# Token order of attention and column order of the dense layers in a four-stage transformer kernel

## The chip, the cores and the metric

The kernel runs on one core of a Trainium2 chip. The metric is the device time of one execution in microseconds. All inputs lie in the chip's memory when it starts, and the result (8 sequences of 512 tokens by 512 features, float32) lies there when it ends.

## What is computed

Four layers follow one another, each on `x` of shape (8, 512, 512): a stencil layer, an attention block with its feed-forward part, an expert layer whose weights are picked by a token of the sequence, and a low-rank correction. Only the second to the fourth matter here; of the stencil nothing changes. Cut to that:

```python
# attention, with a bias for every head and a mask
x = _ln(src) * (1.0 + scale) + shift
q = (x @ Wq + bq).reshape(B, S, 16, 32).transpose(0, 2, 1, 3)      # k, v alike
scores = einsum('bhqd,bhkd->bhqk', q / sqrt(32), k) + attention_bias
scores = where(src_mask, -inf, scores)
ctx = einsum('bhqk,bhkd->bhqd', softmax(scores), v).transpose(0, 2, 1, 3).reshape(B, S, D)
x = x + (ctx @ Wo + bo)
# its feed-forward part: 512 -> 2048 -> 512
h = _ln(x) * g2 + beta2
x = x + (_gelu2(h @ W1 + b1) @ W2 + b2)
# expert layer: the same shape, weights of expert e of the sequence
o = gelu(x @ Wi[e] + bi[e]) @ Wo[e] + bo[e]
y = _ln(o + x) * gamma[e] + beta[e]
# correction: rank 32, with a gate from the mean over the tokens
out = y + strength * ((y @ basis) @ basis.T[:, :32] @ resp_w.T + resp_b + safety_bias)
```

The bias is (8, 16, 512, 512) float32, 134 MB, and is read once. The mask is one byte for each query and key.

## The kernel before

The program has one stage after the other: `stencil`, `attention`, `feed_forward` (expert=False), `feed_forward` (expert=True, with the correction in its `tail`). Each stage writes `x` to memory and the next reads it. Every engine has its own stream of instructions, written out by hand, and they meet by semaphores alone: no scheduler moves anything. P is 128, S and D are 512, R = 4 blocks of tokens, C = 4 blocks of features.

**Token order.** `rows_at` (line 84) loads and stores a sequence as "(p r)": partition p holds tokens 4p to 4p+3, one contiguous run of 8 KB. A transpose on TensorE of block r gives 128 columns, which are tokens r, r+4, r+8 and so on. `by_row` (line 72) is a view of a 512-column tile with a step of 4 elements (16 bytes) between neighbours. Before the change the engines that empty the transposes from PSUM write through it, so that columns stand in the tokens' natural order, and whoever needs the 128 tokens of block r again reads with the step of 4: as the stationary operand of a matmul, or as a transpose's input.

**Attention**, a loop over 8 sequences. `transposes_x` brings x to features by tokens, VectorE writes `xT` with scale and shift (line 1048), ScalarE and VectorE split it into a high part `xH` and a rest `xL` (a product of three fp32r matmuls stands for one in float32: `split_matmul`, lines 91 to 93). Projections q, k, v follow. q and k are made in 4 chunks of 4 heads; SyncE copies each head's high and low parts into `q3` and `k3`, 96 partitions deep. Then come 64 units (u), each one head and one block r of 128 queries, 16 units to a chunk:

- `scores` (TensorE, line 875): one matmul, the stationary operand is `by_row(q3)` of block r, 96x128, moving `k3`, 512 columns. It is issued two units ahead.
- GpSimd has added the mask to the bias of two units (line 723); SyncE loads the bias of two units, 512 KB, in one transfer (line 649) into one of four buffers.
- `sum_scores` (VectorE, line 993), `exp` (ScalarE, line 775), four transposes (TensorE, line 883), `probs_high` (ScalarE, line 782), `probs_low` (VectorE, line 999), `values` (TensorE, line 896, for two units at once).

At unit 8 of the next chunk (u = 24, 40, 56, and after the last unit) the finished chunk is closed: `ctx_high` (ScalarE, line 797) writes `cH` and `ctx_low` (VectorE, line 1025) writes `cL`, both with the step of 4; ScalarE's next instructions, `copy_low` (line 791) and with it the `exp` behind, wait for `cL`. After the units come the output projection, its transposes back (line 942, input `by_row(xT)`) and the store.

In the middle of a sequence, when the second chunk of q and k is being copied, `prefetch` loads x (1 MB) and the mask (256 KB) of the next sequence through the same queue.

**feed_forward**, again 8 sequences of 16 steps f. `transposes` fill PSUM, `h_out` (ScalarE, lines 1450 and 1452) writes `h32` with the step of 4 (by_row), VectorE splits it. A step is `hidden` (12 matmuls, stationary weights) and `output` of the step before (12 matmuls into four banks; the stationary operand is block r of `gH` or `gL`, read with the step of 4). In the expert stage the `tail` of the sequence before runs along: transposes of y (line 1582), `yH` (ScalarE, line 1472) and `yL` (VectorE, line 1821), both written with the step of 4, and the last matmuls (line 1605) with `feats` read with the step of 4. Transposes m and m+1 use one bank, so transpose m+1 waits for `yL` m.

## Time and profile before

| | us |
|---|---|
| median of 3 runs | 3721.76 |
| lowest, highest | 3713.49, 3722.09 |
| the profiled execution | 3728.08 |
| its span, first to last instruction | 3726.3 |
| mean granted clock of TensorE | 0.921 |
| TensorE busy (matmuls) | 3054.0, 82% |
| TensorE weight loads | 2531.2, 68% |
| VectorE busy | 2138.4, 57% |
| ScalarE busy | 1225.2, 33% |
| GpSimd busy | 895.2, 24% |
| DMA | 352.04 MB, 94 GB/s |

The stencil takes the first 225 us, attention goes to 1940 us, the first feed_forward to 2745 us, the expert stage to the end.
### The profile page before, as it was taken

What the parts mean: (1) busy time and instruction counts of PE and PEld (TensorE: products, weight loads), DVE (VectorE), ACT (ScalarE), POOL (GpSimd) and SP (SyncE); (2) the same over time, 40 slices, a digit from 0 to 9 for tenths busy, and PEclk for the clock granted to TensorE, in tenths of its full rate; (3) what the DMA queues carried; (4) which work ended last, traced back from release to release, by engine and by line L of the source; (5) the groups of instructions that cost most, each with busy time, mean ns of one, the idle gap of its engine ahead of it and who ended that gap; (6) DMA issues with size and microseconds to landing.
All of it is one profiled execution on the core that took longest, in us unless ns stands there. A gap on an engine that the chain in (4) does not pass through costs nothing. (4 is left out here: it accounts for less than half of the span.)

```text
span 3726.3 us, 45793 instructions
## 1 busy us (share of the span) xinstructions
PE 3054.0 (82%) x14000; PEld 2531.2 (68%) x14000; DVE 2138.4 (57%) x3930; ACT 1225.2 (33%) x2286; POOL 895.2 (24%) x573
## 2 busy tenths in 40 slices
PE   7938787777777787778769999999979898889886
PEld 4426666666666566666658888988867787778775
DVE  8946667575756667575754444334346465545543
ACT  1116556463636455464611111111111121121121
POOL 1013424142424324242421000000023122211210
PEclk9969899888989899889989999999979999999997
DMA  4235344342525344443422000000034323323310
GB/s 147 95 109 153 111 136 140 117 139 80 159 89 158 97 136 128 128 142 105 139 89 63 23 23 12 11 23 23 12 103 142 102 83 99 102 88 100 94 52 28
DMA packets 204298, 352.04 MB, mean 94 GB/s; under 512 B 25546, under 2 KB 100234, under 8 KB 199306
## 3 DMA queue, kind: packets, MB, share of 16 engines
q1 hardware_dynamic: 202330, 345.96, 30.1%
q0 software_dynamic: 1712, 2.93, 0.3%
q8 instruction: 127, 2.08, 0.2%
q14 instruction: 129, 1.06, 0.1%
HBM read 264.45 MB, written 34.01 MB: 80 GB/s over the span
## 5 line engine op out<-in xcount | busy, mean ns | idle before, releaser
L723 POOL TENSOR_TENSOR at_bias<-at_bias,at_mask 128x1024 f32<-128x1024 f32 x256 | 556.4, 2182 | 1034.2 <-DMA at_bias<-in_fside_Bx16xSxS 1033.8
L883 PE MATMUL at_bank_probT<-at_ident,at_y 128*128 128x128 f32 x2048 | 349.6, 298 | 174.5 <-ACT at_y L775 174.2
L993 DVE CUSTOM_DVE_ANT_0 at_bias<-at_bias,at_bank_score 128x512 f32<-128x512 f32 x512 | 349.6, 684 | 244.1 <-PE at_bank_score L875 146.2
L775 ACT ACTIVATE at_y<-at_bias,at_nmax 128x512 f32<-128x512 f32 x512 | 369.3, 721 | 272.0 <-DVE at_nmax L993 269.1
L883 PEld LDWEIGHTS at_bank_probT<-at_ident,at_y 128*128 128x128 f32 x2048 | 266.6, 153 | 259.6 <-ACT at_y L775 231.9
L896 PE MATMUL at_bank_ctx<-at_pH,at_v 128*64 128x256 f32 x1024 | 291.0, 313 | 104.2 <-DVE at_pL L999 100.0
L999 DVE TENSOR_TENSOR at_pL<-at_bank_probT,at_pH 128x512 fp32r<-128x512 f32 x512 | 352.5, 688 | 28.2 <-ACT at_pH L782 24.5
L875 PE MATMUL at_bank_score<-at_k,at_q 96*128 96x512 f32 x512 | 314.2, 616 | 15.4 <-DMA at_k<-at_nat 15.4
L782 ACT ACTIVATE at_pH<-at_bank_probT 128x512 fp32r<-128x512 f32 x512 | 300.7, 587 | 70.5 <-PE at_bank_probT L883 67.2
L1704 DVE CAST ff_gH<-ff_g 128x512 fp32r<-128x512 f32 x128 | 68.2, 532 | 437.4 <-ACT ff_g L1460 437.2
L1460 ACT ACTIVATE ff_g<-ff_bank_hid,ff_b1c 128x512 f32<-128x512 f32 x128 | 88.2, 689 | 657.8 <-PE ff_bank_hid L93 657.8
L1460 ACT ACTIVATE expert_g<-expert_bank_hid,expert_b1c 128x512 f32<-128x512 f32 x128 | 88.2, 689 | 654.2 <-PE expert_bank_hid L93 654.2
L1386 POOL TENSOR_SCALAR expert_WH<-expert_stage 128x1024 fp32r<-128x1024 f32 x128 | 148.9, 1163 | 611.9 <-PE expert_bank_out L93 476.7
L896 PE MATMUL at_bank_ctx<-at_pL,at_v 128*64 128x256 f32 x1024 | 279.5, 302 | 0.0
L896 PEld LDWEIGHTS at_bank_ctx<-at_pH,at_v 128*64 128x64 f32 x1024 | 150.8, 147 | 180.8 <-DVE at_pL L999 121.1
L1704 DVE CAST expert_gH<-expert_g 128x512 fp32r<-128x512 f32 x128 | 66.6, 520 | 302.8 <-ACT expert_g L1460 302.8
L91 PE MATMUL expert_bank_out<-expert_WH,expert_gH 128*128 128x512 f32 x512 | 210.8, 412 | 13.5 <-DVE expert_gL L1706 13.5
L91 PE MATMUL ff_bank_hid<-ff_hH,ff_WH 128*128 128x512 f32 x512 | 208.1, 407 | 7.0 <-DVE ff_hL L1698 2.6
L91 PE MATMUL expert_bank_hid<-expert_hH,expert_WH 128*128 128x512 f32 x512 | 204.8, 400 | 6.1 <-DVE expert_hL L1698 4.1
L92 PE MATMUL expert_bank_out<-expert_WL,expert_gH 128*128 128x512 f32 x512 | 205.4, 401 | 0.0
L91 PE MATMUL ff_bank_out<-ff_WH,ff_gH 128*128 128x512 f32 x512 | 204.9, 400 | 0.0
L93 PE MATMUL expert_bank_out<-expert_WH,expert_gL 128*128 128x512 f32 x512 | 204.5, 400 | 0.0
(306 smaller groups left out, 6887.4 us busy)
## 6 DMA issues: line engine op xcount, KB each, us to landing
at_bias<-in_fside_Bx16xSxS SPq DMA_DIRECT2D x256, 512.0 KB, 4.2
expert_stage<-in_L_cond_Wi SPq DMA_DIRECT2D x128, 256.0 KB, 2.8
expert_stage<-in_L_cond_Wo SPq DMA_DIRECT2D x128, 256.0 KB, 2.9
at_q<-at_nat SPq DMA_DIRECT2D x384, 64.0 KB, 2.0
at_k<-at_nat SPq DMA_DIRECT2D x384, 64.0 KB, 2.6
st_f<-in_x SPq DMA_DIRECT2D x8, 1024.0 KB, 7.4
x_after_layer<-st_y SPq DMA_DIRECT2D x8, 1024.0 KB, 4.8
at_x<-x_after_layer SPq DMA_DIRECT2D x8, 1024.0 KB, 8.0
```

Source lines behind the costliest of these rows:

```text
L91: pe.matmul(out, wh, xh, start=first, stop=False)
L92: pe.matmul(out, wh, xl, start=False, stop=False)
L93: return pe.matmul(out, wl, xh, start=False, stop=last)
L723: pool.tensor_tensor(bias[i % NB][:, :, :], bias[i % NB][:, :, :], mask[:, 2 * i % R:2 * i % R + 2, :], ALU.add).then_inc(s_bm, 1)
L775: act.activation(prob[u % 2][:, :], bias[u // 2 % NB][:, u % 2, :], ACT.Exp, scale=-1.0, bias=nmax[:, u % 4:u % 4 + 1], accum_out=sums[:, ...
L782: act.activation(pH[u // 2 % 2][:, :, u % 2, :], pT[u % 2][:, :].rearrange("p (k q) -> p k q", q=P), ACT.Copy).then_inc(s_pth, 1)
L875: pe.matmul(pS[u % 2][:, :], by_row(q3[:, j, :])[:, r, :], k3[:, j, :], start=True, stop=True).then_inc(s_qk, 1)
L883: t = pe.transpose(pT[u % 2][:, k * P:(k + 1) * P], prob[u % 2][:, k * P:(k + 1) * P], ident[:, :])
L896: t = pe.matmul(pC[h % 2][0:2 * HD, half * 2 * P:(half + 1) * 2 * P], v[:, k, h, :], probs[i % 2][:, k], start=(k == 0 and g == 0), stop=( ...
L993: dve.tensor_tensor_reduce(t, t, pS[u % 2][:, :], -1.0, 3.0e38, ALU.add, ALU.min, nmax[:, u % 4:u % 4 + 1]).then_inc(s_max, 1)
L999: dve.tensor_tensor(pL[u // 2 % 2][:, :, u % 2, :], pT[u % 2][:, :].rearrange("p (k q) -> p k q", q=P), f32(pH[u // 2 % 2][:, :, u % 2, :] ...
L1460: act.activation(g32[f % 2][:, :], pg[f % 2][:, :], ACT.Gelu if expert else ACT.Gelu_apprx_sigmoid, bias=b1c[:, slot if expert else 0, f:f ...
```

## The change

Attention takes its tokens in another order: `tokens_at` loads and stores x as "(r p)", so that partition p of block r holds token 128r + p. The bias and the mask, whose query rows lie on the same partitions, are loaded in the same order. A transpose of block r then gives 128 columns that already are the tokens' natural order, and all views with a step of 4 in attention become plain slices.

`feed_forward` keeps loading and storing by `rows_at`. Its columns now stay as the transposes leave them, block after block, instead of being put in natural order; since every later step takes whole blocks, nothing else depends on the order. Here too all views with the step become plain slices.

No instruction is added, removed or moved on any engine: each of the five has the same rows in the same order before and after. What differs is the steps in the operands of these instructions, and the pieces of these transfers: the bias moves in 2 KB pieces instead of 4 KB, x of attention in 2 KB instead of 8 KB, the mask in 512-byte pieces instead of 2 KB. The number of bytes stays. Line numbers after line 88 grow by 5, and by 4 and 3 near the end.

```diff
+def tokens_at(x, n):
+
+    return x[ds(n, 1)].rearrange("a (r p) n -> (a p) r n", r=R)
...
-                    sp.dma_start(x[:, :, :], rows_at(x_in, 0)).then_inc(s_x, 16)
-                    sp.dma_start(m8[:, :, :], a["mask_Bx1xSxS_bk0"][0].rearrange("a (p r) k -> (a p) r k", r=R)).then_inc(s_m8, 16)
+                    sp.dma_start(x[:, :, :], tokens_at(x_in, 0)).then_inc(s_x, 16)
+                    sp.dma_start(m8[:, :, :], a["mask_Bx1xSxS_bk0"][0].rearrange("a (r p) k -> (a p) r k", r=R)).then_inc(s_m8, 16)
...
-                sp.dma_start(bias[i % NB][:, :, :], a["fside_Bx16xSxS_0"][ds(n, 1), h].rearrange("a (p r) k -> (a p) r k", r=R)[:, r:r + 2, :]).then_inc(s_bias[i % NB], 16)
+                sp.dma_start(bias[i % NB][:, :, :], a["fside_Bx16xSxS_0"][ds(n, 1), h].rearrange("a (r p) k -> (a p) r k", r=R)[:, r:r + 2, :]).then_inc(s_bias[i % NB], 16)
...
-                sp.dma_start(rows_at(x_out, n), y[:, :, :]).then_inc(s_st, 16)
+                sp.dma_start(tokens_at(x_out, n), y[:, :, :]).then_inc(s_st, 16)
...
-                act.activation(by_row(cH[:, c, :]), pv[:, :].rearrange("d (r p) -> d r p", r=R), ACT.Identity,
+                act.activation(cH[:, c, :], pv[:, :], ACT.Identity,
...
-                pe.matmul(pS[u % 2][:, :], by_row(q3[:, j, :])[:, r, :], k3[:, j, :],
+                pe.matmul(pS[u % 2][:, :], q3[:, j, r * P:(r + 1) * P], k3[:, j, :],
...
-                        t = pe.transpose(out[:, m * P:(m + 1) * P], by_row(xT[:, m, :])[:, r, :], ident[:, :])
+                        t = pe.transpose(out[:, m * P:(m + 1) * P], xT[:, m, r * P:(r + 1) * P], ident[:, :])
...
-                dve.scalar_tensor_tensor(by_row(cL[:, c, :]), pv[:, :].rearrange("d (r p) -> d r p", r=R), bc[:, 3, c:c + 1],
-                                         by_row(f32(cH[:, c, :])), ALU.add, ALU.subtract).then_inc(s_cl, 1)
+                dve.scalar_tensor_tensor(cL[:, c, :], pv[:, :], bc[:, 3, c:c + 1],
+                                         f32(cH[:, c, :]), ALU.add, ALU.subtract).then_inc(s_cl, 1)
...
-                    dve.tensor_scalar(by_row(xT[:, m, :]), pJ[m % 2][:, :].rearrange("d (r p) -> d r p", r=R),
+                    dve.tensor_scalar(xT[:, m, :], pJ[m % 2][:, :],
...
-                    out = by_row(h32[m % 2][:, :])
-                    src = pt[m % 2][:, :].rearrange("d (r p) -> d r p", r=R)
+                    out, src = h32[m % 2][:, :], pt[m % 2][:, :]
...
-                    act.activation(by_row(yH[m % 2][:, :]), pt[0][:, :].rearrange("d (r p) -> d r p", r=R), ACT.Identity,
+                    act.activation(yH[m % 2][:, :], pt[0][:, :], ACT.Identity,
...
-                    gh = gH[f % 2][:, :].rearrange("d (p r) -> d r p", r=R)[:, r, :]
-                    gl = gL[f % 2][:, :].rearrange("d (p r) -> d r p", r=R)[:, r, :]
+                    gh = gH[f % 2][:, r * P:(r + 1) * P]
+                    gl = gL[f % 2][:, r * P:(r + 1) * P]
...
-                    ft = feats[:, :].rearrange("d (p r) -> d r p", r=R)[:, r, :]
+                    ft = feats[:, r * P:(r + 1) * P]
...
-                    dve.tensor_tensor(by_row(yL[m % 2][:, :]), pt[0][:, :].rearrange("d (r p) -> d r p", r=R),
-                                      by_row(f32(yH[m % 2][:, :])), ALU.subtract).then_inc(s_yl, 1)
+                    dve.tensor_tensor(yL[m % 2][:, :], pt[0][:, :], f32(yH[m % 2][:, :]), ALU.subtract).then_inc(s_yl, 1)
```

The transfers of the next sequence's x and mask in `prefetch` change in the same way as the first ones.

## Rows read from the trace of the kernel before

**Rows 1.** Stretches: length, busy time by engine, TensorE's clock, DMA share, GB/s.

```profile
225.00:1940.00 1715.00, 1289.79 (x6625) 1038.55 (x6626) 1107.79 (x2167) 883.85 (x1837) 605.20 (x301) 0.88 0.42 126
1940.00:2745.00 805.00, 753.92 (x3384) 683.08 (x3384) 331.38 (x796) 120.51 (x155) 84.59 (x76) 0.98 0.09 29
2745.00:3726.00 981.00, 829.02 (x3545) 722.28 (x3545) 522.18 (x730) 187.23 (x275) 193.30 (x143) 0.93 0.29 90
```

**Rows 2.** Weight loads by line and form: busy us, mean ns, idle before.

```profile
L875 PEld LDWEIGHTS at_bank_score<-at_k,at_q 96*128 96x128 f32 x512 | 159.3, 312 | 19.2 <-DMA at_k<-at_nat 18.9
...
L92 PEld LDWEIGHTS ff_bank_out<-ff_WL,ff_gH 128*128 128x128 f32 x512 | 158.6, 310 | 0.1
...
L92 PEld LDWEIGHTS ff_bank_hid<-ff_hL,ff_WH 128*128 128x128 f32 x512 | 98.9, 193 | 20.0
```

**Rows 3.** Timeline, first feed_forward: start us, us, engine, line; first matmuls of series.

```profile
2206.74 0.40 PE L91 MATMUL ff_bank_hid<-ff_hH,ff_WH 128*128 128x512 f32 x1
...
2209.47 0.40 PE L91 MATMUL ff_bank_out<-ff_WH,ff_gH 128*128 128x512 f32 x1
...
2212.29 0.40 PE L91 MATMUL ff_bank_hid<-ff_hH,ff_WH 128*128 128x512 f32 x1
```

**Rows 4.** VectorE's and ScalarE's groups by line and form, columns as in Rows 2.

```profile
L1025 DVE SCALAR_TENSOR_TENSOR at_cL<-at_y,at_bc,at_cH 128x512 fp32r<-128x512 f32 x32 | 57.8, 1806 | 10.3 <-ACT at_cH L797 10.1
L981 DVE SCALAR_TENSOR_TENSOR at_nat<-at_bank_proj,at_bc,at_nat 128x512 fp32r<-128x512 f32 x64 | 47.9, 749 | 75.5 <-ACT at_nat L764 75.5
...
L1048 DVE TENSOR_SCALAR at_xT<-at_bank_proj,at_adab 128x512 f32<-128x512 f32 x32 | 36.5, 1181 | 16.4 <-issue 12.9 <-PE at_bank_proj L841 3.3 <-DVE at_adab L1040 0.2
...
L1821 DVE TENSOR_TENSOR expert_yL<-expert_bank_tr,expert_yH 128x512 fp32r<-128x512 f32 x32 | 34.8, 1087 | 11.9 <-ACT expert_yH L1472 11.9
...
L764 ACT ACTIVATE at_nat<-at_bank_proj,at_bc 128x512 fp32r<-128x512 f32 x64 | 43.9, 685 | 76.6 <-PE at_bank_proj L93 76.6
L797 ACT ACTIVATE at_cH<-at_y,at_bc 128x512 fp32r<-128x512 f32 x32 | 38.9, 1216 | 12.3 <-DVE at_y L1021 12.3
...
L1450 ACT ACTIVATE expert_h<-expert_bank_tr 128x512 f32<-128x512 f32 x32 | 33.8, 1122 | 94.0 <-PE expert_bank_tr L1530 91.3 <-DVE expert_hL L1698 2.7
```

**Rows 5.** Timeline where the first chunk of sequence 3 is closed.

```profile
962.98 2.14 POOL L723 TENSOR_TENSOR at_bias<-at_bias,at_mask 128x1024 f32<-128x1024 f32 x1 [2.37 <-DMA at_bias<-in_fside_Bx16xSxS]
963.14 2.92 DVE L1025 SCALAR_TENSOR_TENSOR at_cL<-at_y,at_bc,at_cH 128x512 fp32r<-128x512 f32 x1
...
966.64 0.70 ACT L775 ACTIVATE at_y<-at_bias,at_nmax 128x512 f32<-128x512 f32 x1
```

**Rows 6.** The instructions of line 1025: duration ns min/median/max, starts.

```profile
L1025 DVE SCALAR_TENSOR_TENSOR at_cL<-at_y,at_bc,at_cH x32: 1129/1158/2977, 348.4 to 1873.5; 128x512 fp32r<-128x512 f32 x32
```

**Rows 7.** Timeline: a matmul of 512 columns that follows small ones, twice.

```profile
999.79 0.60 PE L875 MATMUL at_bank_score<-at_k,at_q 96*128 96x512 f32 x1
...
2201.07 0.48 PE L91 MATMUL ff_bank_hid<-ff_hH,ff_WH 128*128 128x512 f32 x1
```

**Rows 8.** Who waited for the matmuls of line 875: us, times.

```profile
  DVE at_bias L993: 146.2, 147
```

**Rows 9.** Timeline, start of a sequence: VectorE's first two `xT`.

```profile
1086.10 2.20 DVE L1048 TENSOR_SCALAR at_xT<-at_bank_proj,at_adab 128x512 f32<-128x512 f32 x2 [3.24 <-issue]
```

**Rows 10.** Timeline: transposes that waited for what empties their bank.

```profile
2020.12 0.66 PE L1530 MATMUL ff_bank_tr<-ff_ident,ff_xn 128*128 128x128 f32 x4 [0.91 <-ACT ff_h L1452]
...
3144.27 0.66 PE L1582 MATMUL expert_bank_tr<-expert_ident,expert_x 128*128 128x128 f32 x4 [1.30 <-DVE expert_yL L1821]
...
3702.16 1.12 PE L1582 MATMUL expert_bank_tr<-expert_ident,expert_x 128*128 128x128 f32 x4 [2.25 <-DVE expert_yL L1821]
```

**Rows 11.** Transfers by tile: count, KB each, median us from issue to landing.

```profile
at_bias<-in_fside_Bx16xSxS SPq DMA_DIRECT2D x256, 512.0 KB, 4.2
expert_stage<-in_L_cond_Wi SPq DMA_DIRECT2D x128, 256.0 KB, 2.8
expert_stage<-in_L_cond_Wo SPq DMA_DIRECT2D x128, 256.0 KB, 2.9
```

More of the change, by code:

```diff
@@ L666, in prefetch @@
                 sp.sem_inc(s_passed, 1)
-                sp.dma_start(x[:, :, :], rows_at(x_in, n + 1)).then_inc(s_x, 16)
-                sp.dma_start(m8[:, :, :], a["mask_Bx1xSxS_bk0"][ds(n + 1, 1)].rearrange("b a (p r) k -> (b a p) r k", r=R)).then_inc(s_m8, 16)
+                sp.dma_start(x[:, :, :], tokens_at(x_in, n + 1)).then_inc(s_x, 16)
+                sp.dma_start(m8[:, :, :], a["mask_Bx1xSxS_bk0"][ds(n + 1, 1)].rearrange("b a (r p) k -> (b a p) r k", r=R)).then_inc(s_m8, 16)
             steps = [(2 * (i - NB) + 2.5, load_bias, (i,)) for i in range(NB, NP)]
```

## The prediction, made before the change was run

> **What bounds the kernel now.** I read the stretches first, then the groups by form, then timelines where one engine waits. The two feed_forward stages belong to TensorE: in the first it is busy for 754 of 805 us at a clock of 0.98 [rows 1], and matmuls follow one another without a break. Attention takes 1715 us, 46% of the span, and there no engine is full (TensorE 75%, VectorE 65%, ScalarE 52%) [rows 1]: it is a chain that passes from engine to engine within a unit. A stride thus costs something only where its instruction sets the pace (feed_forward) or where the chain stands still until it has ended (attention).
>
> **What the step of 4 costs one instruction.** The trace has each kind both ways. A weight load of 128 columns with the step takes 310 ns (312 for the scores), without it 193 [rows 2]. VectorE writes `xT` from PSUM in 1181 ns, while line 981 does the like without the step in 749; ScalarE takes 1216 ns for `cH` and 1122 for `h32`, and 685 for line 764 [rows 4]. So I take 120 ns off a load, 0.43 us off `xT` and 0.5 us off ScalarE's instructions. For `yL` (1087 ns) and `cL` I take 0.4 us. All ends of the terms below start from these.
>
> The Trainium skill (SBUF — State Buffer, Door 1) says that SBUF has lines of 16 bytes and that an access which crosses into a new one each time pays. It also calls a stride of 4 float32 free, which would leave all of this at zero and the time at that of before; the pairs above speak for the first half of its sentence.
>
> **1. feed_forward, `output`.** Twelve `hidden` matmuls start at 2206.74 and the first `output` one at 2209.47: 2.73 us. The twelve of `output` take from there to 2212.29: 2.82 us [rows 3]. The load with the step lies behind the matmul before it except for 0.09/12 = 7.5 ns. 256 steps f of twelve: 256 x 0.09 = 23 us. 24 of the steps wait for `yL` and lose nothing by this; 22 us remain. Bounds: 0 (the pace comes from the change of bank and not from the load) and 23.
>
> **2. Closing a chunk.** 32 times `cH`, then `cL`, and in 24 of them `exp` waits behind; in the other 8 the output projection does. `cL` takes 1158 ns in the median, but 1806 on average [rows 4, 6]; 32 x 0.65 = 21 us are thus in the few that take up to 2977. The timeline shows what these are: GpSimd began its mask sum at 962.98, `cL` at 963.14, it took 2.92 us, and `exp` came at 966.64 [rows 5]. With `cH` shorter by 0.5, `cL` begins at 962.6, ahead of GpSimd, whose start hangs on a transfer. Then such a `cL` costs 0.75 instead of 2.92, 2.2 us less. 21/1.8 = 11.5, so 11 of the 32 are of this kind: 11 x (0.5 + 2.2) = 30 us, the other 21 x (0.5 + 0.4) = 19 us. Together 49. Bounds: 32 x 0.4 = 13 us if every `cL` still ends with GpSimd's sum, and 49.
>
> The Trainium skill (SBUF — State Buffer, Who interferes with whom) has it that a VectorE instruction with two SBUF inputs and a GpSimd one that reads SBUF exclude each other for the whole of the one that began first. By that rule it is the order of the two starts, not the stride, that decides, as in the sum above; where `cL` still comes second, the rule gives back the lower bound.
>
> **3. Scores.** After small matmuls a load isn't covered: the record of `scores` is 0.60 us, that of a 512-column matmul without the step in the same position 0.48 [rows 7]. 0.12 us for each of 512 at most: 61 us. But it counts only where VectorE waits for the scores, and it did 147 times [rows 8]; elsewhere VectorE or ScalarE is behind. 147 x 0.12 = 18, less those at the half clock, where a load is covered more easily (clock 0.88 on average, so about a quarter of attention [rows 1]): 14 us. Bounds: 0 and 61.
>
> **4. Start of a sequence.** `xT` 0 and 1 take 2.20 us back to back [rows 9], and `xT` 2 too lies ahead of the q projection, whose bank it frees: 3 x 0.43 x 8 = 10 us. The fourth is hidden by the projection at half clock. Bounds 0 and 14.
>
> **5. Turns between sequences in feed_forward.** The third transpose waited 0.91 us for ScalarE's `h32`, the fourth alike [rows 10]: with 0.5 less each, 1 us x 8 in the first stage, and half of it in the second, where transposes run at the half clock: 12 us. Three transposes of y in a sequence wait 1.30 us for `yL` [rows 10], which is last behind the split of gelu and of the weights on VectorE; `yH` is done earlier. 21 x 0.4 = 8 us. After the last sequence nothing covers the chain, transposes wait 2.25 us [rows 10]: 4 x (0.5 + 0.4) = 4 us. Together 24, bounds 12 and 24.
>
> **6. The transposes of the output and `feats`** read without the step too: some 2 us, bounds 0 and 5.
>
> **7. Transfers.** Pieces get smaller, bytes stay. The nearest rows: 256 KB in 512-byte pieces (`Wi`) land in 2.8 us, 256 KB in 2 KB pieces (`Wo`) in 2.9 [rows 11]. So the mask and the bias should take no longer. They matter where VectorE waits for a bias, above all behind the 1.25 MB of `prefetch`, 7 times; I put 0.4 us each against the change, 3 us, since the long pieces of x have no counterpart. Bounds: 0, and the price in the last rival.
>
> **Sum**: 22 + 49 + 14 + 10 + 24 + 2 - 3 = 118 us. The profiled execution took 3728.1, so 3610; the median of the runs is 6.3 us below it, so **3604** for the median. The clock is left as it is: shorter stalls in attention should not lower it.
>
> **Rivals.**
> - *The loop gives it back.* GpSimd still comes first at `cL`, the scores' 0.12 us end in VectorE's own work and the smaller pieces cost double. Then terms 2, 3 and 7 are 13, 0 and -8: 22 + 13 + 10 + 24 + 2 - 8 = 63 us, **3659**. For it speaks that VectorE and ScalarE are busy for half of attention, and that both starts hang on the same `exp`; against it, that the lead of GpSimd was 0.16 us and `cH` loses three times that.
> - *TensorE is the chain in every unit.* Then the scores give all of 61 instead of 14 and `xT` 14: 118 + 47 + 4 = 169 us, **3553**. For it: VectorE waited for scores in more than a quarter of the units, and the transposes and `values` behind them in TensorE's queue move too. Against it: `exp` and `probs_low` are more often what TensorE waits for.
> - *The stride isn't the cause*, and the change does not do what it is said to: loads and writes stay as long since another property of these instructions makes them slow. The pairs in rows 2 and 4 differ in tiles too. Time as before, **3722**.
> - *Slower: small pieces stop the SyncE queue.* Copies of q and k share it with the bias. From 256 to 512 KB a landing grows by 4.2 - 2.9 = 1.3 us [rows 11], so 512 KB hold the queue for 2.6. If a byte costs twice as much in small pieces, the three bias transfers among the copies of each of 24 chunks add 7.8 us, and `prefetch` adds 6.4 us 7 times: 187 + 45 = 232 us, less the 118: **3836**. It turns to slower once a byte costs half as much again. Against it stands that `Wi`'s 512-byte pieces are no slower than `Wo`'s.
>
> **How the numbers follow.** Forecast 0.58 (3580 to 3635), the loop gives it back 0.22, TensorE in every unit 0.12, stride not the cause 0.03, slower 0.03, and 0.02 for a gain between 0 and 40 us. To hold 8 in 10 the range takes in the forecast and the first rival and reaches towards the second: **3560 to 3670**. About 0.3% (11 us) is what a measurement of this kernel can tell from no change. Faster by more: 0.94. Within: 0.03. Slower: 0.03.
>
> **What would show it.** Weight loads of `scores` and of `output` near 190 ns, and twelve `output` matmuls in 2.73 us: term 1. `cH` at 0.7, `cL` at 0.75 with hardly any above 2 us: term 2; if the long ones stay in number, the first rival. VectorE's wait for the scores down by 14 us or by far more: term 3. `xT` at 0.75, `h32` at 0.6 to 0.7, `yL` at 0.7. Bias landings still near 4.2 us, else the last rival. What would make it wrong is a stall in attention that stands just behind the one removed: the copies of q and k at a chunk's start hold the first units of it, and they don't get shorter; a gain well below 49 us in the sequences' loops with all durations as said would mean that.

## The result and the profile after

| | before | after |
|---|---|---|
| median of four runs, us | 3721.93 | 3616.76 |
| lowest, highest | 3713.49, 3722.40 | 3610.97, 3633.11 |
| profiled execution | 3728.08 | 3619.43 |

The ratio is 0.973 with a 95% interval of 0.9695 to 0.9765: 105 us less, where 118 had been forecast and 3604 us for the median. The time lies 13 us above the forecast and inside its range of 3560 to 3670.

Where it went, by stage. A stage runs here from its first GpSimd instruction to that of the next (the cuts in rows 1 were rounder: the first 46 us of feed_forward stood in attention's stretch). Columns: stretch, length, busy time of TensorE, its weight loads, VectorE, ScalarE and GpSimd (with instructions), TensorE's granted clock, DMA share, GB/s. The kernel before:

```profile
224.90:1893.60 1668.70, 1262.96 (x6528) 1016.23 (x6528) 1083.23 (x2133) 875.83 (x1829) 583.04 (x279) 0.89 0.42 126
1893.60:2730.60 837.00, 776.69 (x3456) 702.35 (x3456) 354.16 (x824) 127.15 (x161) 97.98 (x77) 0.97 0.10 31
2730.60:3726.30 995.70, 833.08 (x3568) 725.34 (x3568) 523.96 (x736) 188.60 (x276) 202.14 (x163) 0.93 0.29 92
```

and the changed kernel:

```profile
225.90:1833.60 1607.70, 1176.57 (x6528) 933.75 (x6528) 1058.60 (x2133) 858.51 (x1829) 579.31 (x280) 0.91 0.45 130
1833.60:2650.60 817.00, 763.50 (x3456) 628.43 (x3456) 353.94 (x824) 113.75 (x161) 98.25 (x78) 0.97 0.11 32
2650.60:3617.70 967.10, 814.64 (x3568) 647.13 (x3568) 514.32 (x736) 160.31 (x276) 200.71 (x163) 0.93 0.30 94
```

Attention lost 61 us, feed_forward 20, the expert stage 28.6. The groups of the changed kernel that answer to rows 2 and 4 (busy us, mean ns of one, idle time before them and its cause):

```profile
L880 PEld LDWEIGHTS at_bank_score<-at_k,at_q 96*128 96x128 f32 x512 | 105.5, 206 | 22.0 <-DMA at_k<-at_nat 21.4
...
L97 PEld LDWEIGHTS ff_bank_out<-ff_WL,ff_gH 128*128 128x128 f32 x512 | 96.2, 188 | 19.9
...
L1030 DVE SCALAR_TENSOR_TENSOR at_cL<-at_y,at_bc,at_cH 128x512 fp32r<-128x512 f32 x32 | 38.5, 1204 | 6.3 <-ACT at_cH L802 6.3
...
L1019 DVE COPY at_y<-at_inv 128x512 f32<-128x512 f32 x32 | 29.1, 908 | 1.1
...
L1053 DVE TENSOR_SCALAR at_xT<-at_bank_proj,at_adab 128x512 f32<-128x512 f32 x32 | 25.1, 804 | 17.9 <-issue 17.5 <-PE at_bank_proj L846 0.2 <-DVE at_adab L1045 0.2
...
L802 ACT ACTIVATE at_cH<-at_y,at_bc 128x512 fp32r<-128x512 f32 x32 | 22.9, 715 | 12.3 <-DVE at_y L1026 12.3
L1825 DVE TENSOR_TENSOR expert_yL<-expert_bank_tr,expert_yH 128x512 fp32r<-128x512 f32 x32 | 21.9, 684 | 10.4 <-ACT expert_yH L1476 10.4
```

Loads went from 312 and 310 ns to 206 and 188, `cH` from 1216 to 715, `xT` from 1181 to 804, `yL` from 1087 to 684: what a single instruction saves was forecast to within 0.06 us. Only `cL` stands out, with a mean of 1204 where 750 was expected. Its instructions by duration (min/median/max in ns) show that the typical one is short and the long ones are still there:

```profile
L1030 DVE SCALAR_TENSOR_TENSOR at_cL<-at_y,at_bc,at_cH x32: 740/750/2734, 348.4 to 1813.6; 128x512 fp32r<-128x512 f32 x32
```

By the timeline 7 of them take more than 2 us; there were 11.

### The profile page after: what moved, and what is told of

It reads as the page before. It is cut to its first block and busy times, and to the rows that moved or that the text cites. A ratio compares the mean times of both kernels' runs of the same rounds, so it can differ in the third digit from the quotient of the medians.

```text
span 3617.7 us, 45793 instructions
## 1 busy us (share of the span) xinstructions
PE 2936.1 (81%) x14000; PEld 2296.7 (63%) x14000; DVE 2104.3 (58%) x3930; ACT 1166.1 (32%) x2286; POOL 890.2 (25%) x573
## 5 line engine op out<-in xcount | busy, mean ns | idle before, releaser
L998 DVE CUSTOM_DVE_ANT_0 at_bias<-at_bias,at_bank_score 128x512 f32<-128x512 f32 x512 | 348.8, 682 | 215.6 <-PE at_bank_score L880 124.7
L880 PE MATMUL at_bank_score<-at_k,at_q 96*128 96x512 f32 x512 | 258.8, 508 | 17.8 <-DMA at_k<-at_nat 17.7
L96 PE MATMUL expert_bank_hid<-expert_hH,expert_WH 128*128 128x512 f32 x512 | 204.2, 399 | 7.0 <-DVE expert_hL L1702 4.7
L98 PE MATMUL ff_bank_hid<-ff_hH,ff_WL 128*128 128x512 f32 x512 | 204.6, 400 | 0.0
L97 PE MATMUL ff_bank_hid<-ff_hL,ff_WH 128*128 128x512 f32 x512 | 204.3, 399 | 0.0
```

The lines of the kernel that those rows point to most:

```text
L96: pe.matmul(out, wh, xh, start=first, stop=False)
L97: pe.matmul(out, wh, xl, start=False, stop=False)
L98: return pe.matmul(out, wl, xh, start=False, stop=last)
L880: pe.matmul(pS[u % 2][:, :], q3[:, j, r * P:(r + 1) * P], k3[:, j, :], start=True, stop=True).then_inc(s_qk, 1)
L998: dve.tensor_tensor_reduce(t, t, pS[u % 2][:, :], -1.0, 3.0e38, ALU.add, ALU.min, nmax[:, u % 4:u % 4 + 1]).then_inc(s_max, 1)
```

## Why GpSimd still came first

The prediction said that with `cH` shorter by 0.5 us `cL` would begin 0.5 us earlier. The kernel before, at the place of rows 5, shows what that left out:

```profile
961.88 1.23 ACT L797 ACTIVATE at_cH<-at_y,at_bc 128x512 fp32r<-128x512 f32 x1
...
962.54 0.69 DVE L999 TENSOR_TENSOR at_pL<-at_bank_probT,at_pH 128x512 fp32r<-128x512 f32 x1
```

`cH` ends at 963.11, but VectorE itself is busy with the `pL` that stands ahead of `cL` in its queue, and `cL` follows it at 963.14. Two things hold `cL`, and they end together. In the changed kernel at the same place only the queue is left:

```profile
936.15 0.71 ACT L802 ACTIVATE at_cH<-at_y,at_bc 128x512 fp32r<-128x512 f32 x1
...
936.69 0.69 DVE L1004 TENSOR_TENSOR at_pL<-at_bank_probT,at_pH 128x512 fp32r<-128x512 f32 x1
937.29 2.71 DVE L1030 SCALAR_TENSOR_TENSOR at_cL<-at_y,at_bc,at_cH 128x512 fp32r<-128x512 f32 x1
...
937.31 2.14 POOL L728 TENSOR_TENSOR at_bias<-at_bias,at_mask 128x1024 f32<-128x1024 f32 x1 [2.79 <-DMA at_bias<-in_fside_Bx16xSxS]
...
940.59 0.70 ACT L780 ACTIVATE at_y<-at_bias,at_nmax 128x512 f32<-128x512 f32 x1
```

`cH` is done at 936.86 and `cL` begins 0.43 us later. It loses to GpSimd although its record begins 0.02 us earlier. One sequence on, the lead is 0.06 us and it wins; now GpSimd's sum takes 2.69 us instead of 2.14:

```profile
1133.91 0.74 DVE L1030 SCALAR_TENSOR_TENSOR at_cL<-at_y,at_bc,at_cH 128x512 fp32r<-128x512 f32 x1
...
1133.97 2.69 POOL L728 TENSOR_TENSOR at_bias<-at_bias,at_mask 128x1024 f32<-128x1024 f32 x1 [3.55 <-DMA at_bias<-in_fside_Bx16xSxS]
```

The rule of the Trainium skill (SBUF — State Buffer, Who interferes with whom), that whoever starts first has the shared port for the whole instruction, agrees with both places if a lead of 0.02 us in the records is taken as a tie.

## The experiments

For the parts of attention I compare with the mean of three profiles in which attention is the same (the changed kernel, `dense_old` and `output_step4`: 1607.7, 1619.1 and 1605.4 us, mean 1610.7). An effect below some 10 us in a single stage time of attention is thus not told, and the kernel before has one profile to compare with, 1668.7 us. The feed_forward stages repeat better: 812.5 to 819.0 and 963.6 to 970.0 us over all kernels in which they are as changed. "Loops" is the sum over 8 sequences from the first `exp` to the end of the last, "between" the sum of the 7 stretches from there to the next sequence's first `exp`.

### Which part gives what, taken back one at a time

**dense_old**: the whole `feed_forward` function of the kernel before, attention as changed.

> Attention as changed, both feed_forward stages as before the change; the output is the reference's. If the stages do not influence each other, attention stays at 1607.7, the stages go back to 837.0 and 995.7, and the whole takes 48.6 us more than the changed kernel, 3668. If the time of attention moves by more than 2 us here, stage times can't be compared that finely between profiles.

Measured: 3671.24 us, ratio to before 0.9883 (0.9848 to 0.9919), 54 us above the changed kernel; stages 1619.1, 831.5 and 990.4. Over the four kernels with the old dense stages these take 835.3 and 991.8 us on average, with the new ones 814.9 and 967.1: the dense part is worth 20.4 + 24.7 = 45 us by the stages. Attention moved by 11 us with nothing changed in it, which the text had named as the sign that single stage times there can't be read to 2 us.

**output_step4**:

```diff
-                    gh = gH[f % 2][:, r * P:(r + 1) * P]
+                    gh = gH[f % 2][:, :].rearrange("d (p r) -> d r p", r=R)[:, r, :]
```

and `gl` alike.

> The changed kernel with only the stationary operand of output, in both feed_forward stages, read with the step of 4 again; the rows of the output are then other tokens than those of x. Term 1: 0.09 us in each of 256 steps, 11.5 us in each stage but for the 24 steps of the second that wait for yL: the stages at 828.5 and 977.5 us from 817.0 and 967.1. If the load is hidden and the change of bank makes the pace: within 1 us of 817.0 and 967.1.

Measured (one run): 830.9 and 970.5 us, so 16.0 and 3.4 us against those means, 19.4 together where 22 was forecast. The 3.4 us lie just outside the spread of that stage, so that the split between the stages is rough. The load, back at 310 ns, isn't fully hidden in either stage: the starts of neighbouring `output` matmuls are 237 ns apart in the median in both, against 227 in the changed kernel. In the first the price is larger than forecast, in the second most of it disappears: there TensorE waits in other places as well. That a slower `output` shortens those waits is my reading; no run shows it by itself.

**scores_step4**, **xT_step4** and **close_step4**: one view with the step back in each.

```diff
-                pe.matmul(pS[u % 2][:, :], q3[:, j, r * P:(r + 1) * P], k3[:, j, :],
+                pe.matmul(pS[u % 2][:, :], by_row(q3[:, j, :])[:, r, :], k3[:, j, :],
...
-                    dve.tensor_scalar(xT[:, m, :], pJ[m % 2][:, :],
+                    dve.tensor_scalar(by_row(xT[:, m, :]), pJ[m % 2][:, :].rearrange("d (r p) -> d r p", r=R),
...
-                act.activation(cH[:, c, :], pv[:, :], ACT.Identity,
+                act.activation(by_row(cH[:, c, :]), pv[:, :].rearrange("d (r p) -> d r p", r=R), ACT.Identity,
```

(in `close_step4` also `cL`).

> The changed kernel with only the scores' stationary operand read with the step of 4 again, so the rows of the scores belong to other tokens than the bias. Term 3 of the forecast: the weight load goes back from 206 to about 310 ns and attention gets 14 us longer (1622). If TensorE is the chain in every unit: 61 us or more (1669). If the wait ends in VectorE's own queue: attention stays within 3 us of 1607.7.

> The changed kernel with only xT written with the step of 4 again, so that q, k and v have their tokens in another order than the bias. Term 4 of the forecast: three of the four count, 0.43 us each, 8 times: 10 us, attention 1618. If all four count and the projections behind them also run at the lower clock for longer: 14 us and more. Between the loops, the stretch from the first to the last xT took 5.43 before and 4.32 us after.

> The changed kernel with only cH and cL written with the step of 4 again, so the output projection has its columns in another order than xT. If each closing stands in the path with its whole length: cH 0.5 and cL 0.4 longer in 32 closings, 29 us, and attention 1637. If cL still ends with GpSimd's sum where it comes second, in 8 of them, and those lose only 0.5: 25 us. If as much as the forecast's term 2, with three more collisions: 36 us, 1644. A stall behind it that takes the time up (the bias behind the prefetch, in the chunk where 8 of the closings stand): 15 us or less.

**pieces_4k**: `rows_at` instead of `tokens_at`, "(p r)" for the bias and the mask.

> The changed kernel with attention's five transfers in the old order (token p*4+r on partition p, pieces of 4 KB for the bias, of 8 KB for x and y); everything on the engines is as changed. The bias and mask then belong to other tokens than the scores. Theory 1, the small pieces cost time behind the prefetch: VectorE's wait for the bias of the second chunk's fourth unit, which grew from 6.13 to 7.24 us in sequence 3, goes back to about 6.1, and attention gets 7 to 9 us shorter than the 1607.7 us of the changed kernel. Theory 2, that wait is set by the bytes in the queue and grew only because the loop now reaches it earlier: attention stays at 1607.7 within 2 us, the wait stays near 7.2 us. The forecast had put 3 us on the pieces.

| kernel | time, us | attention, against 1610.7 | loops, against 1178.5 | between, against 340.6 | `cL` over 2 us |
|---|---|---|---|---|---|
| changed kernel | 3616.8 | -3 | -3 | -1 | 7 |
| scores_step4 | 3632.0 | +11 | +12 | -1 | 10 |
| xT_step4 | 3645.7 (one run) | +24 | +8 | +13 | 5 |
| close_step4 | 3663.3 | +47 | +31 | +15 | 13 |
| pieces_4k | 3633.1 | +6 | +8 | -2 | 11 |
| all of attention (kernel before) | | +58 | +27 | +28 | 11 |

The closing costs 47 us when it is taken back, about the 49 of term 2 and more than any reading of the expectation allowed (36 at most). The scores cost 11 (15 by the medians) against 14, and TensorE isn't the chain in every unit. `xT` costs 24 in its one profile instead of 10. The small pieces do not cost anything that is seen here: with the old ones attention is not shorter, and the medians are 16 us longer. The first theory asked for a wait near 6.1 us in sequence 3 and got 6.3 instead of 7.2, but with the small pieces that wait is 5.3 us in `dense_old` and 7.4 in `output_step4`, so it tells nothing. But the four add up to 88 us, and all together are worth 58. In the stretches between loops they add (13 + 15 = 28), in the loops they do not (59 against 27).

### The same parts added to the kernel before

**old_close_plain** and **old_scores_plain**: the edits of `close_step4` and `scores_step4` the other way round, on the kernel before.

> The kernel before with one part of the change alone: cH and cL written without the step, so the output projection has its columns in another order than xT. Undoing this part in the changed kernel cost 47 us of attention. If the parts add, attention falls from 1668.7 to about 1622 and the time by 47 us. If they overlap in the loops of the sequences (undone one at a time they cost 31, 12 and 8 us there, together they gave 27), whoever comes first takes most: the loops fall from 1205 to 1179 or less and the stretches between them by 15 us, 41 us in all or more, and nothing is left in the loops for the other parts. If the clock is what couples them, half-clock time falls from 372 to about 310 us.

> The kernel before with only the scores' stationary operand read without the step; the rows of the scores belong to other tokens than the bias. Undone in the changed kernel this part cost 11 us of attention, 15 us of the median. If the parts add: attention 1655 to 1658. If a stall of the closings or of the bias takes the time up in the kernel before: attention 1665 to 1672, no gain.

| kernel | time, us | ratio, 95% interval | attention, against 1668.7 | loops | between | `cL` over 2 us |
|---|---|---|---|---|---|---|
| old_close_plain | 3705.5 | 0.9958, 0.9937 to 0.9979 | -26 | -9 | -16 | 13 |
| old_scores_plain | 3710.7 | 0.9973, 0.9947 to 0.9998 | -4 | 0 | -2 | 13 |

For the closing none of my three readings held. Its medians give 15 us, with 8 to 23 in the interval, and the profile 26; neither is 47 or 41, and the time at the half clock in attention fell from 372 to 332 us, not to 310. For the scores the second reading, no gain, holds by the profile (1665.0), while the medians of ten runs give 10 us. Whoever comes first doesn't take most: the closing alone takes 9 us off the loops, while taking it back from the changed kernel costs 31. The timeline shows what stands in its way:

```profile
955.43 2.14 POOL L723 TENSOR_TENSOR at_bias<-at_bias,at_mask 128x1024 f32<-128x1024 f32 x1 [1.54 <-DMA at_bias<-in_fside_Bx16xSxS]
...
955.65 2.47 DVE L1025 SCALAR_TENSOR_TENSOR at_cL<-at_y,at_bc,at_cH 128x512 fp32r<-128x512 f32 x1
```

Here `cH` ends at 955.10, but VectorE gets through its queue only at 955.65, 0.55 us later, since the `sum_scores` ahead of it waits for a matmul with the slow load. GpSimd is 0.22 us ahead. With both parts the lag is 0.43 us and the starts nearly coincide. The slow load is one thing that settles who gets the port at `cL`: in `scores_step4` the lag is 0.55 us too, and all eight first-chunk closings are long (4 to 6 of the eight in the three profiles with the attention as changed). The pieces of the transfers are another, which I had overlooked. In `pieces_4k` the lag is 0.43 us, as in the changed kernel, but GpSimd starts 0.01 to 0.15 us ahead in all eight, and all eight are long; at the same place as above:

```profile
940.51 2.13 POOL L728 TENSOR_TENSOR at_bias<-at_bias,at_mask 128x1024 f32<-128x1024 f32 x1 [1.69 <-DMA at_bias<-in_fside_Bx16xSxS]
...
940.66 2.54 DVE L1030 SCALAR_TENSOR_TENSOR at_cL<-at_y,at_bc,at_cH 128x512 fp32r<-128x512 f32 x1
```

So three parts of the change act on one race. How much the closing and the scores give together on the kernel before was not run. The totals of `cL` are, in us: 57.8 before [rows 4], 48.2 with the closing alone, 38.5, 38.2 and 36.0 in the three profiles with the attention as changed, 41.5 with the scores taken back, 46.1 with the pieces, 61.1 with the closing. Adding `cH` (32 x 0.5 = 16 us each time) gives 16 + 10 = 26 us for the closing alone, which is what its profile says and more than its medians do, and 16 + 23.5 = 39.5 of the 47 for the closing taken back.

With the scores alone the time goes elsewhere. VectorE's waits for scores and for biases together fall from 232.9 to 217.0 us, 16 less, while `cL` takes 4.3 more, the copy of the inverses (line 1014) 6.6 more and the multiplications of line 965 1.8 more.

### Without any collision at cL

**cL_first**:

```diff
+                    if u % UC == 8 and u > UC:
+                        ctx_low(n, u // UC - 1)
                     if u > 0:
                         probs_low(n, u - 1)
                     if u - 1 in after:
                         low(n, after[u - 1])
                     if u % UC == 8 and u > UC:
-                        ctx_low(n, u // UC - 1)
                         add_high(n, u // R - 2)
```

> The changed kernel with one edit of order: in the unit where a chunk is closed, VectorE does cL before the pL of the unit before, so that it begins as soon as cH has ended, some 0.4 us ahead of GpSimd's sum, instead of 0.02 us around it. The output is the reference's. Theory, the order of the two starts decides: no cL above 1.2 us, eight times 2.0 us less, and pL comes 0.8 us later at 24 closings, of which some reaches TensorE: attention 10 to 16 us shorter than 1607.7. Rival 1, the order doesn't decide and any overlap blocks VectorE: eight cL still take 2.6 to 2.7 us. Rival 2, the collision goes but the bias behind the prefetch or the next pL takes the time up: cL short, attention within 3 us of 1607.7.

Measured: 3618.13 us, ratio 0.9712 (0.9671 to 0.9753), the same as the changed kernel; attention 1607.5. No `cL` is long any more, but VectorE's multiplications of `x` by `rstd` (line 970) grow and its wait for GpSimd's sum is longer. `cL_first`, two groups and a wait (us, times, longest):

```profile
L970 DVE TENSOR_SCALAR at_x<-at_x,at_mv,at_rstd 128x512 f32<-128x512 f32 x32 | 30.6, 1018 | 1.2 <-POOL at_rstd L710 1.2
...
L1030 DVE SCALAR_TENSOR_TENSOR at_cL<-at_y,at_bc,at_cH 128x512 fp32r<-128x512 f32 x32 | 25.8, 805 | 9.4 <-ACT at_cH L802 6.5
...
DVE at_bias L998 <- POOL at_bias L728: 90.4, 26, 7.9
```

The changed kernel:

```profile
L970 DVE TENSOR_SCALAR at_x<-at_x,at_mv,at_rstd 128x512 f32<-128x512 f32 x32 | 24.3, 823 | 1.2 <-POOL at_rstd L710 1.2
...
DVE at_bias L998 <- PE at_bank_score L880: 124.7, 114, 6.4
DVE at_bias L998 <- POOL at_bias L728: 79.5, 24, 7.2
```

The first theory holds for the port: the order of the starts decides. For the time rival 2 fits: against the means of the three profiles with the attention as changed, `cL` lost 11.8 us (37.6 to 25.8), while line 970 took 4.5 more (26.1 to 30.6), the copy of line 1019 3.6 more (30.7 to 34.3) and the wait for a bias 7.9 more (82.5 to 90.4). The last is within what these three show among themselves, 79.5, 91.7 and 76.3 us. Taken together with the wait for scores it is 214.7 us against 204.2, 208.5 and 205.0, which is outside. That these put the gain back on the chain isn't shown by them. I looked at the wait for the bias, the largest of the three.

### The stall behind: a bias that comes late

In the changed kernel VectorE stands still in unit 20 of sequence 3 until GpSimd has masked a bias:

```profile
924.83 0.69 DVE L998 CUSTOM_DVE_ANT_0 at_bias<-at_bias,at_bank_score 128x512 f32<-128x512 f32 x1 [7.24 <-POOL at_bias L728]
```

**split_prefetch**: four rows of x and the mask as five transfers, each behind the bias of another unit, instead of `if k == 8` for all of it.

```diff
-                    if k == 8 and not last:
-                        prefetch(n)
+                    if k in parts and not last:
+                        prefetch(n, parts.index(k))
```

with `parts` the steps at units 4, 8, 22, 24 and 38, and **split_cL_first**, the same with `cL` ahead.

> The changed kernel with the prefetch of the next sequence in parts: the four 256 KB rows of x behind the bias of units 4, 8, 22 and 24, the mask behind that of unit 38, instead of 1.25 MB at once near unit 12. The output is the reference's. Theory, the wait of VectorE for the bias in unit 20 of a sequence (4.8 to 7.2 us, 7 times, where the eighth sequence has no prefetch) is this transfer standing ahead of the bias in the queue: it falls to 1 us or less, attention 28 to 40 us shorter than 1611 (mean of three profiles of the same attention), the time near 3585. Rival, the queue is late anyway since copies of q and k hold it: the wait moves to a later unit and attention stays above 1600.

> The split prefetch and cL ahead of pL together; the output is the reference's. cL ahead of pL alone took 12 us out of cL and gave none of it to the whole. If it was the late bias that took it up, it shows here: 8 to 12 us below the split prefetch alone. If it is the order of VectorE's queue itself (pL and values come 0.8 us later in 24 closings), the two kernels are within 3 us of each other.

Measured: 3583.66 us (ratio 0.9633, 0.9595 to 0.967), attention 1577.0, and 3582.97 us (0.9629, 0.9588 to 0.9669), attention 1571.8. The prefetch was the wait of unit 20: it is gone, and with it 33 us of the time, although the copy of the inverses grew from 30.7 to 44.9 us and the wait of unit 18 from 16 to 20. Putting `cL` ahead is worth 1 us by the medians and 5 by the profile, within the noise; my 8 to 12 us failed here too.

What remained were waits in units 18, 34 and 50, where a chunk of q and k has just been copied. SyncE's queue in `split_cL_first` (start, us, with the number of issues):

```profile
888.40 0.37 SPq L655 DMA_DIRECT2D at_bias<-in_fside_Bx16xSxS  x1
892.79 1.79 SPq L665 DMA_DIRECT2D at_q<-at_nat  x3
894.62 1.86 SPq L665 DMA_DIRECT2D at_k<-at_nat  x3
896.52 1.85 SPq L665 DMA_DIRECT2D at_q<-at_nat  x3
898.66 0.38 SPq L655 DMA_DIRECT2D at_bias<-in_fside_Bx16xSxS  x1
```

Between 888.40 and 898.66 no bias is issued. **bias_queue** lets ScalarE issue the bias loads:

```diff
                     if u > 0:
                         probs_high(n, u - 1)
+                    if u % 2 == 1:
+                        i = u // 2 + NB
+                        if i < NP:
+                            load_bias(act, n, i)
+                        elif not last:
+                            load_bias(act, n + 1, i - NP)
```

> The split prefetch with cL ahead of pL, and in addition the bias loads issued by ScalarE in every second unit behind pH, on the same condition as before, instead of by SyncE, whose queue keeps the copies of q and k and the five parts of the prefetch. The output is the reference's. With the split prefetch VectorE still waits for a bias in units 18, 34 and 50 of each sequence (2.7, 3.0 and 2.4 us, 24 times, some 65 us with the copies of the inverses that GpSimd's same sum holds up). Theory, the bias stands behind the copies of q and k in SyncE's queue, which wait for scores: these waits fall below 20 us in all, attention to 1530 or less from 1571.8, the time to 3545 or less. Rival 1, the transfers themselves are what is late there (copies and bias share the engines): the waits stay within a fifth, the time within 10 us of 3583. Rival 2, ScalarE pays for 256 issues, 0.1 us each: 26 us back, the time near 3570.

Measured: **3521.87 us**, ratio to before 0.9447 (0.9407 to 0.9486), the fastest of all; attention 1515.8. Of VectorE's waits for GpSimd's sum, 63.4 us in `split_cL_first`, nothing is left; all that it waits for there is

```profile
DVE at_bias L1010 <- PE at_bank_score L892: 139.0, 156, 2.4
DVE at_bias L1010 <- issue: 9.2, 11, 3.5
DVE at_bias L1010 <- ACT at_y L786: 1.4, 4, 0.4
```

Not all of the 63.4 us is gained: the wait for scores grew from 113.5 to 139.0, and the copy of the inverses fell from 43.5 to 20.8: 63 - 26 + 23 = 60 us, where attention got 56 shorter. The transfers were not late by their bytes but by their place in the queue. The 252 issues take 0.39 us each in ScalarE's records, 98 us in all and not 26 as the second rival had it, and cost nothing that shows in the sum. The same edit gives the prefetch waits of its own, which was not run apart. The Trainium skill (Trainium Kernel Development and Optimization, Key Constraints) says that issuing from several engines saves only the issue time. Here it saves more, since SyncE's queue is taken in order and the copies in it wait for scores.

## Why the prediction was right or wrong, step by step

**The direction and the size** came out: 105 us where 118 was forecast. Of the dense stages' terms, 22 + 24 + about 1, 45 us were measured; of attention's, 49 + 14 + 10 + 2 - 3 = 72, only 58 to 60. That the sum came within 13 us is in part luck: in the loops 27 us were gained where the terms hold 56, and between them 28 where the terms hold some 18.

**Term 1, `output`: 22, measured 19.** The reading from the starts was right; the sum has a slip, since 24 steps of 0.09 less leave 21 and not 22. In the changed kernel twelve `output` matmuls, the next twelve `hidden` and what follows start at the same distance, 2.72 us:

```profile
2090.28 0.39 PE L96 MATMUL ff_bank_out<-ff_WH,ff_gH 128*128 128x512 f32 x1
...
2093.00 0.39 PE L96 MATMUL ff_bank_hid<-ff_hH,ff_WH 128*128 128x512 f32 x1
...
2095.72 0.39 PE L96 MATMUL ff_bank_out<-ff_WH,ff_gH 128*128 128x512 f32 x1
```

Over both stages the price was split 16 to 3, not half to half: in the expert stage more is lost in other waits than the 24 steps that the sum had taken out for it.

**Term 5, turns in feed_forward: 24, measured 26** as what is left of the 45 (with the transposes of y and `feats` in it). TensorE's waits of the expert stage before the change,

```profile
PEld expert_bank_tr L1582 <- DVE expert_yL L1821: 38.9, 24, 3.2
...
PEld expert_bank_tr L1530 <- ACT expert_h L1450: 8.7, 16, 1.0
```

and after it,

```profile
PEld expert_bank_tr L1586 <- DVE expert_yL L1825: 32.4, 24, 2.4
...
PEld expert_bank_tr L1534 <- ACT expert_h L1454: 2.7, 8, 0.5
```

account for 12.5 us of it in that stage, against 4 + 8 + 4 of the sum.

**Term 2, closing a chunk: 49. This is the step that failed**, and in it the sentence "with `cH` shorter by 0.5, `cL` begins at 962.6, ahead of GpSimd". `cH` gave its 16 us. `cL` gave 20 (57.8 to a mean of 37.6) instead of 33: 7 long ones stayed of 11, since VectorE's own queue held `cL` as long as `cH` had. Taken back from the changed kernel the closing costs 47 us (`close_step4`), of which some 9 are TensorE's clock between the sequences and not the instructions; by itself it is worth 26 by the profile and 15 by the medians. By its instructions the closing thus gave 36 us in the changed kernel, 13 less than the term, as much as the sum and the measurement differ by; the surplus of term 4 and a rest in the loops, below, cancel. The first rival had the mechanism (GpSimd still first) and took it for all of them; the truth lies between, nearer to it at first chunks, where 6 of 8 were still long.

**Term 3, scores: 14, measured 11 to 15** in the changed kernel. The attention of `scores_step4`, 1622.1 us, is the 1622 of the expectation. VectorE's wait for the scores fell from 146.2 us [rows 8] to 124.7, but this sign doesn't tell the price: with the slow load back it is 120.6, since the profile puts a wait behind both scores and bias down now to one, now to the other. Both together are 232.9 us before, 205.9 in the mean of the three profiles and 215.0 in `scores_step4`. At the half clock, as the sum had it, the load is covered: the record of a `scores` matmul is 775 ns in the median with the step and without, at full clock 594 and 481. The second rival, 61 us, is out. In the kernel before the same edit gives 4 us in the profile and 10 by the medians.

**Term 4, start of a sequence: 10, measured 24 in one profile, of it 13 between the loops.** The 8 us in the loops are within the noise. The `xT` themselves give 0.38 us each, three or four of them 9 to 12 us. What was missing is TensorE's clock, which the prediction had left as it is. From the last `exp` of sequence 3 to the first of sequence 4 it took, before and after (the last one of a sequence in the first row, the first one of the next in the second):

```profile
1055.69 0.72 ACT L775 ACTIVATE at_y<-at_bias,at_nmax 128x512 f32<-128x512 f32 x1 [0.75 <-DVE at_nmax L993]
...
1111.55 0.72 ACT L775 ACTIVATE at_y<-at_bias,at_nmax 128x512 f32<-128x512 f32 x1 [1.59 <-DVE at_nmax L993]
```

```profile
1026.01 0.72 ACT L780 ACTIVATE at_y<-at_bias,at_nmax 128x512 f32<-128x512 f32 x1 [0.56 <-DVE at_nmax L998]
...
1077.00 0.72 ACT L780 ACTIVATE at_y<-at_bias,at_nmax 128x512 f32<-128x512 f32 x1 [1.59 <-DVE at_nmax L998]
```

55.9 against 51.0 us. The shorter instructions, `cH`, `cL` and four `xT`, explain 0.5 + 0.4 + 1.1 = 2.0 of the 4.9. The rest lies in two places: from the first matmul of the output projection to its last addition (10.7 us before, 9.2 after) and from the first q matmul to the `exp` (21.5 and 19.8). These are the same matmuls at another clock: the first 4 us of the output projection behind `cL` and the first 6 of the q projection behind `xT`, before,

```profile
1065.00:1069.00 4.00, 3.89 (x10) 3.12 (x11) 0.80 (x2) 0.00 (x0) 0.00 (x0) 0.57 0.01 2
1090.00:1096.00 6.00, 5.96 (x15) 4.67 (x16) 2.74 (x4) 1.43 (x3) 0.00 (x0) 0.52 0.00 0
```

and after:

```profile
1034.50:1038.50 4.00, 3.92 (x17) 3.25 (x18) 0.95 (x3) 0.00 (x0) 0.00 (x0) 1.00 0.00 2
1057.20:1063.20 6.00, 5.96 (x22) 4.91 (x23) 3.27 (x5) 1.89 (x3) 0.00 (x0) 0.83 0.00 0
```

At 0.57 and 0.52 nearly all of it ran at 1.2 GHz; after the change the output projection ran at 2.4 GHz throughout (17 matmuls instead of 10 in 4 us) and the q projection rose after a few. What stood ahead of the output projection, before and after:

```profile
1065.11 0.79 PE L91 MATMUL at_bank_proj<-at_cH,at_WH 128*128 128x512 f32 x1 [2.08 <-DVE at_cL L1025]
```

```profile
1034.58 0.50 PE L96 MATMUL at_bank_proj<-at_cH,at_WH 128*128 128x512 f32 x1 [1.22 <-DVE at_cL L1030]
```

TensorE stood still for 2.08 us and for 1.22. `close_step4` brings the slow output projection back in 4 of 7 sequences and `xT_step4` a longer stretch of slow q projection in all, hence 15 and 13 us where 6 and 8 (7 x 0.9 and 7 x 1.1) are in the instructions.

**Terms 6 and 7.** The transposes of the output read without the step too, at 140 ns instead of 210; their 2 us can't be told apart. The pieces were forecast at 3 us lost, and no loss was found: `pieces_4k` is 6 us longer in attention and 16 by the medians, on the other side, with 11 long `cL`. If anything the small pieces helped. The rival on the other side, 3836, is out: the landing of a bias stayed at 4.1 us in the median against 4.2 [rows 11].

**The stride isn't the cause** is out as well: each instruction whose step was put back went back to its old duration. The Trainium skill (SBUF — State Buffer, Door 1) calls a stride of 4 float32 free; on every reader and writer here it cost 0.07 to 0.5 us an instruction, so on that the measurement decides against the sentence. Its 16-byte lines would explain the price; no run here tries another step.

**The warning at the end**, that a stall just behind the removed one would show as a small gain in the loops, was the right place to look, but no stall was shown to have grown by as much: the wait for a bias was 86.7 us before and 82.5 after in the mean; whatever it is put down to, VectorE stood still for 39 us before the units 20 and 20 us before the units 18, and for 44 and 16 in the mean after the change. The loops gained 27 us where terms 2 and 3 hold about 56 of them (49 less the 8 closings at the end, 7 us, and 14). 13 of the missing 29 are the long `cL`. Of the other 16 I can't say for certain where they went. The copy of line 1019 took 8 us more than before the change (22.4 to a mean of 30.7), of which the share on the chain is not known; a collision avoided can come back as a longer wait for a bias or in another instruction (`cL_first`), but how much of this change's gain went that way was not shown.

## What to carry to other kernels

An instruction that waits for another engine also waits for its own queue: before a wait is priced by the producer's end, look at when the consumer's engine gets there, for the later of the two holds. Where several parts of a change act on one race, price them together; closing and scores, added one by one, were worth 26 and 4 us (15 and 10 by the medians), taken back one by one 47 and 11 (47 and 15). And when a gain is smaller than its parts, look for the wait with the fewest, longest entries: here bias loads behind other transfers in a queue taken in order were worth 95 us, nearly as much as the whole change.

## What the runs showed that was not expected

- **A lead of 0.02 us does not win the port.** Over all profiles with a plain or stepped `cL`, the one whose record begins up to 0.037 us ahead of GpSimd's always lost (17 cases with leads of 0.002 to 0.040 us, 2.69 to 3.12 us long), from 0.042 us on it always won (0.74), and at 0.038 to 0.040 both happened. The start of a record is thus not exactly the moment that decides, and a race this close turns on a tenth of a microsecond anywhere upstream.
- **Other instructions on VectorE are long too.** The multiplications of line 970 take 0.54 us in the median, but 5 to 7 of 32 take 2.2 to 2.4 us in the three profiles with the attention as changed (7 before the change), and 8 without any collision at `cL`. The copy of line 1019 grew from a mean of 699 ns before the change to 908 after it, and 996 in `output_step4`.
- **The clock behind a stall belongs to its price.** Behind a stall of 1.2 us the output projection began at 2.4 GHz in all seven sequences of the changed kernel. Behind 2.05 to 2.08 us it was at 1.2 GHz in most of its first 4 us in six of seven before the change, and in `close_step4`, with the same stall, in four of seven: the longer stall didn't always end at the lower level. 0.9 us less of standing still came with about 1 us less for the additions behind its matmuls (9.9 against 8.9 us from the first `xT` addition to the last, mean of 7).
- **A load that the records call hidden was not free.** With loads of 310 ns the pace of `output` was 235 ns and without the step it is 227, 8 ns or 4% (2.82 us against 2.72 for twelve) [rows 3].
